# Value products of a pair in one group at beat 4, and another order of the side work, in a fused FFN, attention, FFN block

## The chip, the cores and the metric

One core of a Trainium2 chip. The metric is the device time of one launch in microseconds; smaller is better. The compute engines are TensorE (PE, and PEld for its weight loads), VectorE (DVE), ScalarE (ACT) and GpSimd (POOL); SyncE (SP) issues the DMAs.

## What is computed

Sixteen batches of 512 tokens with 128 channels go through a block of three stages, all in float32:

```python
x = x + 0.5 * ffn(layernorm(x), W_fc, W_proj)
x = x + attention(layernorm(x), w_qkv, w_out, b_out)
x = x + 0.5 * ffn(layernorm(x), W_fc, W_proj)
# attention: 16 heads of 64, q scaled by 1/8, a causal mask, sim - slope[head] * (i - j), softmax
# ffn: y = square(relu(x @ W_fc.T)) @ W_proj.T, then a spiking recurrence on y:
for step in range(5):
    mem = 0.9 * mem + y - (mem > 1)     # mem starts as y
    count += (mem > 1)
return count / 5
```

Layer norm has no weights (eps 1e-5); the output is 16 x 512 x 128 float32.

## The kernel before, in words

Heads are handled in pairs, eight pairs to a batch. The program of every engine is a sequence of *slots*, one for each pair (s = 0 to 7), and a slot has six *beats* (k = 0 to 5). "(s,k)" below means beat k of slot s. Batch 0 and batch 15 are written out; batches 1 to 14 are a hardware loop over two batches, whose body starts with the odd one (`run`, L252).

**In slot s TensorE does three pairs at once.** For pair s it makes the masked score tiles, one beat each (`scores`, L347; TILES, L26: beats 0 and 2 are 512 keys wide, 1 and 3 are 384, beats 4 and 5 hold two tiles of both heads). For pair s-1 it transposes the normalised probabilities in five runs of four 128x128 blocks (`turn`, L363; TBEAT: beats 1, 2, 3, 5, 5). For pair s-2 it makes the value products (`pv`, L378): for each block j of 128 keys, head 0 in array columns 0 to 63 and head 1 in columns 64 to 127, each of (4 - j) * 128 moving columns, all of a pair summed in one PSUM bank. PV (L40) says at which beats. A float32 product is two matmul instructions here, so one j is four of them.

**Side work** is everything else for TensorE: q and k of the next pair, v, the transposes after a layer norm (t1, t2, t3), the two FFN products of the next batch's first FFN (fc1, y1) and of the last batch's second FFN (fc3, y3), and the output projection of the last batch (out). SIDE (L65) lists it as (slot, beat, kind, tile, batch offset). Entry n of the list goes to side bank n % 2. `last_user` (L237) finds for entry n the entry before it with the same parity, and `freed` (L222) names the semaphore that says that the bank has been emptied; `side` (L451) waits for it before the first matmul. 

**Order within a beat k of slot s**, on each engine in program order:

- TensorE (`slot`, L475): the scores of tile k (they wait until VectorE has biased tile k-3, three score banks), the value products of this beat, the transposes of this beat (they wait for POOL's normalisation of the tiles concerned), then the side work of (s,k).
- VectorE (`slot`, L719): waits for the scores of tile k, then the reciprocal of the sums of tile k-2, `bias_max` of tile k (L553), then `low_half` (L666) for the side work of the beat *before*: for q, k, t it subtracts the rounded high half from the bank and stores the low half, for out it adds the residual. Then `steps` (L688): layer norm statistics and normalisation (LN1, LN2, LN3), and the steps of the spike recurrence (SPIKE1, SPIKE3).
- ScalarE (`slot`, L863): `high_half` (L819) for the side work of the beat before (q, k, t: the rounded high half; v, fc, y: the copy out of the bank), the copies of this beat's transposes (`turned_out`, L805), the copy of the finished value products at ATTBEAT (`att_out`, L812), then the exponentials of tile k (`exps`, L789).
- POOL (`slot`, L926): the multiplication of tile k-2 with the reciprocals (`norm`), and the squares of fc tiles.

So the bank of a v, fc or y is free after ScalarE's copy at the next beat; the bank of a q, k, t or out after VectorE's `low_half` at the next beat, which stands behind the wait for that beat's scores:

```python
if exists(b, s):
    bias_wait(b, s, k)          # dve.wait_ge(s_scores, tile_no(b, s, k))
last = (b, s, k - 2) if k >= 2 else (*before(b, s, 1), BEATS + k - 2)
if exists(*last[:2]):
    recip(*last)
if exists(b, s):
    bias_max(b, s, k)
...
for n, kind, i, off, ss in side_at(s, k - 1, offsets):
    low_half(n, kind, i, b + off, ss, (par + off) % 2)
steps(b, s, k, par, offsets)
```

SyncE copies the halves of q and k between partitions as soon as they are there (`place`, L289), for the pair of the next slot.

Of the kernel before, what the change touches and what calls it, by code (L numbers as in the profile page):

```python
# [35 lines left out]
TNEEDS = [max(SEG_TILE[h, i] for h, j in runs for i in range(j, NT)) for runs in TRUNS]  # L36
TRING = 8
TBEAT = [1, 2, 3, 5, 5]
ATTBEAT = 4
PV = [[2], [], [1, 3], [], [0], []]  # L40
PVORDER = [j for js in PV for j in js]

PVLAST = [max(PVORDER.index(j) for _, j in runs) for runs in TRUNS]
# [12 lines left out]
def beats_from(slot, beat, counts):  # L56

    at = [divmod(slot * BEATS + beat + n, BEATS) for n in range(len(counts))]
    return [x for x, c in zip(at, counts) for _ in range(c)]
# [3 lines left out]

SIDE = [  # L65
# [11 lines left out]
]  # L77

SPIKE1 = beats_from(3, 0, [2, 3, 1, 1, 0, 0, 1, 1, 1, 1, 2, 1])
SPIKE3 = beats_from(6, 3, [1, 2, 2, 1, 2, 1, 2, 1, 2])  # L80
LN1 = dict(stats=(0, 0), aggregate=(0, 1), rstd=(0, 1), normalise=(0, 3))
LN2 = dict(stats=(5, 2), aggregate=(5, 3), rstd=(5, 3), normalise=(6, 1))
LN3 = dict(stats=(3, 4), aggregate=(3, 5), rstd=(3, 5), normalise=(4, 0))

def macaron_kernel(nc: bass.Bass, x, w_qkv, w_out, b_out, w_fc, w_proj, out):
    ctx = ExitStack()
    with ctx:
# [251 lines left out]
        def _(pe):  # L340
# [134 lines left out]
            def slot(b, s, par, offsets, between=None):  # L475
                t_of, pv_of = before(b, s, 1), before(b, s, 2)
                for k in range(BEATS):
                    if exists(b, s):
                        scores(b, s, k, par)
                    for j in PV[k]:  # L480
                        if exists(*pv_of):
# [65 lines left out]
        def _(dve):  # L547
# [140 lines left out]
            def steps(b, s, k, par, offsets):  # L688

                if 1 in offsets:  # L690
                    nb, npar = b + 1, 1 - par
                    if (s, k) == LN1["stats"]:
                        dve.wait_ge(s_xin[npar], (nb - npar) * 8 + 16)
                        stats_of(1, x_in[:, npar, :, :], nb)
                    if (s, k) == LN1["normalise"]:
                        normalise(1, x_in[:, npar, :, :], nb)
                    for n in range(spike_ops):
                        if (s, k) == SPIKE1[n]:
                            spike_step(1, nb, n)
                    if (s, k) == SPIKE1[spike_ops]:  # L700
                        finish1(nb, npar)
# [4 lines left out]
                if -1 in offsets:  # L706
# [4 lines left out]
                    for n in range(spike_ops):  # L711
                        if (s, k) == SPIKE3[n]:
                            spike_step(3, b - 1, n)
                    if (s, k) == SPIKE3[spike_ops]:
                        finish3(b - 1)

            AGGREGATE = [(LN1["aggregate"], 1, 1), (LN3["aggregate"], 3, -1), (LN2["aggregate"], 2, 1)]

# [69 lines left out]
        def _(act):  # L788
# [74 lines left out]
            def slot(b, s, par, offsets):  # L863
                for k in range(BEATS):
                    for n, kind, i, off, ss in side_at(s, k - 1, offsets):
                        high_half(n, kind, i, b + off, ss, (par + off) % 2)
                    for t in range(len(TRUNS)):
                        if TBEAT[t] == k and exists(*before(b, s, 1)):
                            turned_out(*before(b, s, 1), t)
                    if k == ATTBEAT and exists(*before(b, s, 2)):  # L870
                        att_out(*before(b, s, 2), par if s >= 2 else 1 - par)
# [119 lines left out]
```

## Time and profile before

| | us |
|---|---|
| median of 3 runs | 1767.83 (1766.23 to 1768.95) |
| span of the profiled execution | 1764.1 |
| TensorE busy | 1676.8 (95%) |
| ScalarE busy | 1289.0 (73%) |
| VectorE busy | 1206.1 (68%) |
| POOL busy | 920.2 (52%) |
| TensorE on the chain that ended last | 69% |
| VectorE on it | 19% |

Matmuls overlap in the trace: one with 512 moving columns is shown 0.40 us long and adds 0.23 to a stream. How long a piece of work really takes on TensorE is therefore read from where one piece ends and the next ends, as in the chain of waits, and not from the length of an instruction.

### The profile page before, as it was taken

How to read it: one execution, taken by the hardware profiler on the slowest of the kernel's cores; microseconds unless marked ns; L12 is line 12 of the kernel's file. 1: busy time of each engine (PE TensorE's matmuls, PEld its weight loads, DVE VectorE, ACT ScalarE, POOL GpSimd, SP SyncE).
4: the chain of work that ended last, by engine and by line, in shares of the span. 5: the costliest groups of instructions: out<-in, count | busy, mean ns of one | idle time of the engine just before them, and what ended most of it. 6: DMA issues, size and time to landing. Idle time of an engine off the chain costs nothing.

```text
span 1764.1 us, 39796 instructions
## 1 busy us (share of the span) xinstructions
PE 1676.8 (95%) x10902; PEld 1259.1 (71%) x10902; DVE 1206.1 (68%) x4272; ACT 1289.0 (73%) x3446; POOL 920.2 (52%) x1258
## 2 busy tenths in 40 slices
PE   4899999999999999999999999999999999999996
PEld 3767777677776777767777676776777677677775
DVE  6575776748777585775858768586785848767563
ACT  2687876777877787876877768687777868868781
POOL 2455554555545455545555545465454545546451
PEclk8999999999999999999999999999999999999998
DMA  2555453435434435443545434444443544434430
GB/s 73 114 109 111 85 119 75 102 82 109 101 81 107 89 84 108 92 104 76 105 93 107 96 82 107 90 87 107 90 103 78 109 95 94 102 82 101 94 82 13
DMA packets 80562, 164.80 MB, mean 93 GB/s; under 512 B 12880, under 2 KB 30928, under 8 KB 80208
## 3 DMA queue, kind: packets, MB, share of 16 engines
q1 hardware_dynamic: 80336, 162.12, 42.9%
q8 instruction: 101, 1.65, 0.4%
q14 instruction: 125, 1.02, 0.2%
HBM read 6.88 MB, written 4.19 MB: 6 GB/s over the span
## 4 chain that ended last, share of the span: by engine, by line
PE 69%; DVE 19%; issue 8%; POOL 2%; ACT 1%; DVEq 1%; DMA 1%; SPq 0%; POOLq 0%; ACTq 0%
PE bank L388 12%; PE bank L373 12%; PE bank L343 7%; PE bank L359 7%; PE bank L431 7%; PE bank L360 6%; PE bank L439 6%; PE bank L345 5%; PE bank L344 5%; DVE spikes L615 3%; DVE negsc L558 3%; DVE negmem L621 2%; DVE drive L618 2%; DVE xn L591 1%; DVE rsum L567 1%
## 5 line engine op out<-in xcount | busy, mean ns | idle before, releaser
L911 POOL TENSOR_TENSOR prob<-prob,rsum 128x512 f32<-128x512 f32 (+3 forms) x1024 | 731.7, 730 | 699.9 <-DVE rsum L567 699.6
L799 ACT ACTIVATE prob<-negsc,negmax 128x512 f32<-128x512 f32 (+3 forms) x1024 | 574.4, 565 | 124.2 <-DVE negmax L558 117.7
L810 ACT COPY probT<-bank 128x512 f32<-128x512 f32 x640 | 362.0, 587 | 194.5 <-PE bank L373 191.9
L558 DVE CUSTOM_DVE_ANT_0 negsc<-bank,alibi 128x512 f32<-128x512 f32 (+3 forms) x1024 | 466.2, 473 | 5.3 <-PE bank L360 5.3
L567 DVE RECIPROCAL rsum<-sums 128x1 f32<-128x1 f32 (+1 forms) x768 | 121.4, 158 | 483.3 <-PE bank L360 466.3
L373 PE MATMUL bank<-ident,prob 128*128 128x128 f32 x2560 | 373.6, 277 | 1.9 <-ACT probT L810 0.2
L359 PE MATMUL bank<-keys,queries 128*128 128x256 f32 (+2 forms) x1024 | 352.1, 355 | 23.1 <-DVE negmax L558 14.4
L388 PE MATMUL bank<-probT,vals 128*64 128x256 f32 (+3 forms) x2048 | 361.0, 453 | 0.3 <-ACT attT L817 0.3
L373 PEld LDWEIGHTS bank<-ident,prob 128*128 128x128 f32 x2560 | 296.2, 141 | 39.4 <-issue 28.6
L360 PE MATMUL bank<-keys,queries 128*128 128x256 f32 (+2 forms) x1024 | 321.2, 325 | 0.0
L359 PEld LDWEIGHTS bank<-keys,queries 128*128 128x128 f32 x1024 | 194.8, 190 | 74.6 <-DVE negmax L558 30.5
L388 PEld LDWEIGHTS bank<-probT,vals 128*64 128x64 f32 x2048 | 113.0, 135 | 155.9 <-issue 106.0
L360 PEld LDWEIGHTS bank<-keys,queries 128*128 128x128 f32 x1024 | 195.4, 191 | 13.9
L799 ACT ACTIVATION_READ_ACCUMULATOR prob<-negsc,negmax 128x1 f32 x1024 | 199.3, 195 | 0.0
L917 POOL TENSOR_TENSOR hid<-hid 128x512 f32<-128x512 f32 x128 | 136.4, 1077 | 13.8 <-ACT hid L852 13.8
L431 PEld LDWEIGHTS bank<-wproj,hid 128*128 128x128 f32 x1024 | 120.7, 195 | 17.4 <-issue 12.9
L431 PE MATMUL bank<-wproj,hid 128*128 128x128 f32 x1024 | 127.4, 280 | 3.5 <-POOL hid L917 3.5
L615 DVE SCALAR_TENSOR_TENSOR spikes<-negmem,spikes 128x512 f32<-128x512 f32 (+1 forms) x136 | 117.4, 868 | 1.0
L439 PE MATMUL bank<-wo,attT 128*128 128x128 f32 x960 | 114.5, 275 | 0.0
L439 PEld LDWEIGHTS bank<-wo,attT 128*128 128x128 f32 x960 | 110.7, 192 | 0.0
L817 ACT COPY attT<-bank 128x512 f32<-128x512 f32 x128 | 74.9, 585 | 46.0 <-PE bank L388 43.5
L672 DVE TENSOR_TENSOR queries<-bank,queries 128x512 fp32r<-128x512 f32 x128 | 87.4, 683 | 15.6 <-ACT queries L827 14.9
(82 smaller groups left out, 2246.3 us busy)
## 6 DMA issues: line engine op xcount, KB each, us to landing
queries<-queries SPq DMA_DIRECT2D x384, 256.0 KB, 3.0
keys<-k_lo SPq DMA_DIRECT2D x256, 128.0 KB, 2.4
keys<-keys SPq DMA_DIRECT2D x128, 128.0 KB, 3.7
x_in<-in_L_attn_x_dram SPq DMA_DIRECT2D x16, 256.0 KB, 2.9
out_dram<-x SPq DMA_DIRECT2D x16, 256.0 KB, 2.4
prob<-in_L_attn_w_qkv_dram SPq DMA_DIRECT2D x1, 1536.0 KB, 9.1
wo<-in_L_attn_w_out_dram SPq DMA_DIRECT2D x1, 512.0 KB, 10.7
probT<-in_L_ffn_W_fc_dram SPq DMA_DIRECT2D x1, 256.0 KB, 3.2
```

The source lines that it names most:

```text
L359: pe.matmul(dst, q_hi[:, p % 2, h, rows], keys[:, p % 2, h, 0:width], start=True, stop=False)
L360: mm = pe.matmul(dst, q_lo[:, p % 2, h, rows], keys[:, p % 2, h, 0:width], start=False, stop=True)
L373: mm = pe.transpose(turn_bank[n % 2][:, col:col + P], prob[:, p % 2, h, PCOL[i] + j * P:PCOL[i] + (j + 1) * P], ident[:, :])
L388: mm = pe.matmul(pv_bank[h * DH:(h + 1) * DH, j * P:N], vals[:, (p // 2) % 2, j, (p % 2) * P + h * DH:(p % 2) * P + (h + 1) * DH], probT[: ...
L431: mm = pe.matmul(dst[:, t * C:(t + 1) * C], hid[:, i, rows], wproj[:, i, :], start=(i == 0 and t == 0), stop=(i == FC - 1), skip_group_che ...
L439: mm = pe.matmul(dst[:, 0:C], attT[:, att_at(m, par), t * P:(t + 1) * P], wo[:, m, :], start=(m == 0), stop=(m == PAIRS - 1))
L558: ins = dve.tensor_tensor_reduce(negsc[:, k % 3, col:col + WIDTH[i]], src, alibi[:, 2 * p + h, N - WIDTH[i]:N], 1.0, MASKED, ALU.add, ALU.min,
L567: dve.reciprocal(rsum[:, p % 2, cols], sums[:, p % 2, cols]).then_inc(s_rsum, 1)
L615: ins = dve.scalar_tensor_tensor(out=spikes[:, cols], in0=mem[:, cols], scalar=sign * THRESHOLD, in1=spikes[:, cols], op0=fires, op1=ALU.add)
L799: ins = act.activation(prob[:, p % 2, h, PCOL[i]:PCOL[i] + WIDTH[i]], negsc[:, k % 3, col:col + WIDTH[i]], ACT.Exp, bias=negmax[:, p % 2, ...
L810: act.copy(probT[:, turn_slot(p, t), :], turn_bank[(len(TRUNS) * p + t) % 2][:, :]).then_inc(s_turned_out, 1)
L911: ins = pool.tensor_tensor(pr, pr, rsum[:, p % 2, seg:seg + 1].to_broadcast([P, WIDTH[i]]), ALU.mult)
```

## The change

All value products of a pair move to beat 4, in the order of j, and the copy of their sum moves to beat 5. SIDE is written anew: the same kinds and numbers of side products (43 entries before and after), at other beats and in another order; with it move the beats of the layer norms' and the spikes' steps on VectorE and POOL. Sizes, banks, semaphores and arithmetic stay.

```diff
-ATTBEAT = 4
-PV = [[2], [], [1, 3], [], [0], []]
+ATTBEAT = 5
+PV = [[], [], [], [], [0, 1, 2, 3], []]
 SIDE = [
-    (0, 0, "q", 0, 0), (0, 1, "k", 0, 0), (0, 3, "v", 0, 0), (0, 4, "t1", 0, 1), (0, 4, "v", 1, 0),
-    (1, 0, "q", 0, 0), (1, 1, "k", 0, 0), (1, 2, "fc1", 0, 1), (1, 4, "fc1", 1, 1), (1, 4, "fc1", 2, 1),
-    (2, 0, "fc1", 3, 1), (2, 0, "q", 0, 0), (2, 1, "out", 0, -1), (2, 1, "out", 1, -1), (2, 2, "y1", 0, 1),
-    (2, 2, "k", 0, 0), (2, 3, "out", 2, -1), (2, 4, "y1", 1, 1), (2, 5, "v", 0, 0),
-    (3, 0, "v", 1, 0), (3, 0, "q", 0, 0), (3, 1, "k", 0, 0), (3, 2, "out", 3, -1),
-    (4, 0, "k", 0, 0), (4, 0, "q", 0, 0), (4, 2, "t3", 0, -1), (4, 3, "v", 0, 0), (4, 4, "v", 1, 0),
-    (5, 0, "q", 0, 0), (5, 1, "fc3", 0, -1), (5, 2, "k", 0, 0), (5, 4, "fc3", 1, -1), (5, 4, "fc3", 2, -1),
-    (5, 5, "fc3", 3, -1),
-    (6, 0, "q", 0, 0), (6, 1, "k", 0, 0), (6, 2, "y3", 0, -1), (6, 2, "y3", 1, -1), (6, 3, "t2", 0, 1),
-    (6, 4, "v", 0, 0), (6, 5, "v", 1, 0),
-    (7, 0, "q", 0, 1), (7, 1, "k", 0, 1),
+    (0, 0, "q", 0, 0), (0, 1, "k", 0, 0), (0, 2, "v", 0, 0), (0, 5, "v", 1, 0), (0, 5, "t1", 0, 1),
+    (1, 0, "q", 0, 0), (1, 0, "fc1", 0, 1), (1, 1, "k", 0, 0), (1, 1, "fc1", 1, 1), (1, 2, "fc1", 2, 1),
+    (1, 3, "fc1", 3, 1), (1, 5, "y1", 0, 1),
+    (2, 0, "q", 0, 0), (2, 1, "y1", 1, 1), (2, 1, "k", 0, 0), (2, 2, "out", 0, -1), (2, 3, "out", 1, -1),
+    (2, 5, "out", 2, -1),
+    (3, 0, "q", 0, 0), (3, 0, "out", 3, -1), (3, 1, "k", 0, 0), (3, 2, "v", 0, 0), (3, 3, "v", 1, 0),
+    (4, 0, "q", 0, 0), (4, 1, "k", 0, 0), (4, 2, "v", 0, 0), (4, 2, "t3", 0, -1), (4, 3, "v", 1, 0),
+    (4, 5, "fc3", 0, -1),
+    (5, 0, "q", 0, 0), (5, 0, "fc3", 1, -1), (5, 1, "k", 0, 0), (5, 2, "fc3", 2, -1), (5, 3, "fc3", 3, -1),
+    (5, 4, "t2", 0, 1), (5, 5, "y3", 0, -1),
+    (6, 0, "q", 0, 0), (6, 0, "y3", 1, -1), (6, 1, "k", 0, 0), (6, 2, "v", 0, 0),
+    (7, 0, "v", 1, 0), (7, 0, "q", 0, 1), (7, 1, "k", 0, 1),
 ]
-SPIKE1 = beats_from(3, 0, [2, 3, 1, 1, 0, 0, 1, 1, 1, 1, 2, 1])
-SPIKE3 = beats_from(6, 3, [1, 2, 2, 1, 2, 1, 2, 1, 2])
-LN1 = dict(stats=(0, 0), aggregate=(0, 1), rstd=(0, 1), normalise=(0, 3))
-LN2 = dict(stats=(5, 2), aggregate=(5, 3), rstd=(5, 3), normalise=(6, 1))
-LN3 = dict(stats=(3, 4), aggregate=(3, 5), rstd=(3, 5), normalise=(4, 0))
+SPIKE1 = beats_from(2, 3, [1, 1, 2, 1, 1, 0, 1, 1, 1, 0, 1, 1, 2, 1])
+SPIKE3 = beats_from(6, 2, [1, 1, 2, 1, 2, 1, 2, 1, 2, 1])
+LN1 = dict(stats=(0, 0), aggregate=(0, 1), rstd=(0, 1), normalise=(0, 2))
+LN2 = dict(stats=(4, 5), aggregate=(5, 0), rstd=(5, 0), normalise=(5, 2))
+LN3 = dict(stats=(3, 2), aggregate=(3, 3), rstd=(3, 3), normalise=(4, 0))
```

## Rows read from the trace of the kernel before

**Rows 1.** The page: busy time of each engine, and the chain by engine.
```profile
PE 1676.8 (95%) x10902; PEld 1259.1 (71%) x10902; DVE 1206.1 (68%) x4272; ACT 1289.0 (73%) x3446; POOL 920.2 (52%) x1258
PE 69%; DVE 19%; issue 8%; POOL 2%; ACT 1%; DVEq 1%; DMA 1%; SPq 0%; POOLq 0%; ACTq 0%
```

**Rows 2.** Windows, batches 5, 6: length; busy PE, PEld, DVE, ACT, POOL; PEclk, DMA.
```profile
558.33:665.70 107.37, 102.78 (x676) 76.84 (x676) 74.97 (x265) 80.11 (x215) 57.05 (x79) 1.00 0.44 95
665.70:770.96 105.26, 103.17 (x677) 76.78 (x676) 74.85 (x265) 80.09 (x215) 57.04 (x79) 1.00 0.45 96
```

**Rows 3.** The same for slots 0, 4 and 7 of batch 6.
```profile
665.70:679.15 13.45, 11.90 (x76) 8.19 (x75) 11.96 (x47) 10.91 (x32) 8.12 (x12) 1.00 0.63 141
...
722.01:734.05 12.04, 11.50 (x76) 8.19 (x75) 11.70 (x39) 9.70 (x27) 6.81 (x10) 1.00 0.35 75
...
761.25:770.96 9.71, 9.71 (x62) 6.53 (x60) 9.63 (x26) 7.54 (x20) 4.71 (x8) 1.00 0.43 89
```

**Rows 4.** The chain in slot 1 of batch 6: start, length, engine, line, count.
```profile
683.46 1.01 PE bank L388 x8
684.47 0.59 PE bank L373 x4
...
686.10 0.44 PE bank L373 x4
...
687.01 1.01 PE bank L388 x4
688.02 0.43 PE bank L343
688.45 0.23 PE bank L344
```

**Rows 5.** Timeline, slot 1 beat 1: start, length, engine, line, operation, shapes, count.
```profile
681.34 0.34 PE L360 MATMUL bank<-keys,queries 128*128 128x384 f32 x1
...
681.88 0.48 PE L343 MATMUL bank<-xa_hi,wk_hi 128*128 128x512 f32 x1
...
682.26 0.69 DVE L672 TENSOR_TENSOR queries<-bank,queries 128x512 fp32r<-128x512 f32 x1
```

**Rows 6.** Timeline, slot 1 beat 2: last scores matmul, low half of k.
```profile
683.06 0.40 PE L360 MATMUL bank<-keys,queries 128*128 128x512 f32 x1
...
684.17 0.69 DVE L679 TENSOR_TENSOR k_lo<-bank,keys 128x512 fp32r<-128x512 f32 x1
```

**Rows 7.** Timeline, slot 4: a side product (v 1) and what released it.
```profile
731.38 0.68 DVE L684 TENSOR_TENSOR xf_lo<-bank,xf_hi 128x512 fp32r<-128x512 f32 x1
...
732.11 0.39 PE L343 MATMUL bank<-wv_hi,xa_hi 128*128 128x256 f32 x1 [0.43 <-DVE xf_lo L684]
```

**Rows 8.** The chain in batch 8: a tile of y1.
```profile
912.48 1.79 PE bank L431 x16
```

**Rows 9.** Timeline, end of slot 1: last transposes, ScalarE's last read of beat 5.
```profile
689.92 1.03 PE L373 MATMUL bank<-ident,prob 128*128 128x128 f32 x8
...
692.28 0.20 ACT L799 ACTIVATION_READ_ACCUMULATOR prob<-negsc,negmax 128x1 f32 x1
```

**Rows 10.** Timeline of VectorE, slot 4: the normalisation before the second FFN.
```profile
724.61 2.24 DVE L591 TENSOR_SCALAR xn<-x,meanvar,rstd 128x128 f32<-128x128 f32 x4 [0.15 <-POOL rstd L924]
```

**Rows 11.** Lines by form, VectorE: busy us, mean ns of one, idle before.
```profile
L615 DVE SCALAR_TENSOR_TENSOR spikes<-negmem,spikes 128x512 f32<-128x512 f32 x120 | 111.4, 929 | 1.0
...
L649 DVE TENSOR_TENSOR x1b<-x,bias 128x512 f32<-128x512 f32 x16 | 20.5, 1280 | 0.0
```

**Rows 12.** Lines by form, POOL: normalisation of a tile 384 wide.
```profile
L911 POOL TENSOR_TENSOR prob<-prob,rsum 128x384 f32<-128x384 f32 x256 | 211.6, 827 | 305.6 <-DVE rsum L567 305.5
```

**Rows 13.** Timelines of TensorE and of VectorE at the loop's branch (batch 7).
```profile
773.07 0.49 PE L359 MATMUL bank<-keys,queries 128*128 128x512 f32 x1 [2.11 <-DVE negmax L558]
...
777.22 0.17 DVE L567 RECIPROCAL rsum<-sums 128x2 f32<-128x2 f32 x1 [2.63 <-PE bank L360]
```

**Rows 14.** Window just behind that wait: granted clock in the PEclk column.
```profile
774.20:777.60 3.40, 3.40 (x12) 2.83 (x11) 0.77 (x3) 0.00 (x0) 0.13 (x1) 0.50 0.45 123
```

## The prediction

> **What bounds the kernel now.** I read the page first: TensorE is busy for 95% of the span, and its matmuls are 69% of the chain that ended last, VectorE 19% [rows 1]. Next the windows by batch [rows 2]: an even batch takes 105.26 us, an odd one 107.37 (the loop body holds one of each; its branch lies ahead of the odd one). In either, VectorE works 75 us, ScalarE 80. Then the windows by slot of batch 6 [rows 3]: TensorE is idle in slot 0 (11.90 busy of 13.45) and slot 4 (11.50 of 12.04), in slot 7 (9.71 of 9.71) and the other five not. Last, the chain inside a slot [rows 4], where each piece ends where the next begins, so its length is what a matmul really adds. So TensorE's order of work is the bound almost everywhere, and a saving there counts in full, unless the new order makes it wait.
>
> **What the value products save.** A 128-column weight tile is followed by 64-column ones at each group. The group at beat 4 (four matmuls, two heads side by side, four passes of 512 columns at 2.4 GHz, 0.85 us) takes 1.01; the group at beat 2 (384 and 128 columns, the same 0.85) takes 1.01 too [rows 4]. So going in costs 0.15, and the change of width between products of one group costs nothing. Coming out, the next product takes 0.43 where its follower takes 0.23 (0.20 lost), and four transposes take 0.59 where four without a group ahead take 0.44 (0.15 lost) [rows 4]. The change removes the group at beat 0 (0.15 + 0.20, before a side product) and that at beat 2 (0.15 + 0.15, before transposes): 0.65 us a slot. It does so in 128 slots: 83 us, 5.2 a batch. No other TensorE work is added or dropped; the matmuls of a batch then sum to 96.0 us against 101.2 now.
>
> The Trainium skill (TensorEngine Tiling (Array Packing), Key Properties) says that a change of tiling mode drains the array, and its page TensorE: Matmul & The Clock Gate (Part 2, the drain step) puts a drain at some 128 cycles, an estimated 0.05 us at 2.4 GHz. By that, four crossings a slot would give 27 us, not 83. The trace has three to four times that at each crossing, and I go by it.
>
> **What the side work costs.** Side products use two banks in turn: each waits until the side product two places back in SIDE has been emptied (last_user, freed). For q, k, t and out it is VectorE that frees the bank, in low_half, one beat later and behind bias_max, which needs the scores of that later beat. So a side product at beat k+1 whose bank was used by a q at beat k can't start until VectorE has seen scores k+1. Length of that way: the scores of beat 1 end at 681.68 (the last starts 681.34, 0.34 long), VectorE's low half ends at 682.95 [rows 5]: 1.27 us. At beat 2: from 683.46 to 684.86, 1.40 [rows 6]. TensorE meanwhile has only four transposes (0.44) ahead of k. A released product begins 0.06 after the release and its first matmul is seen whole, 0.39 for 256 columns [rows 7] and 0.48 to 0.50 for 512 [rows 5], not the 0.12 (0.23) that it adds in a stream. So k after q: 1.27 + 0.06 + 0.50 + 0.46 = 2.29 after the scores, against 0.44 + 0.70 = 1.14 now: **1.15 us lost**. In the kernel before, k never shares q's bank at one beat's distance: in slot 1 it starts at 681.88, 0.20 after the scores end [rows 5], where the release would let it start at 683.01. In the new SIDE one entry stands between q and k, so they share. Going through the new list:
> - k at (1,1), (3,1), (5,1), (6,1), each behind q at beat 0: 4 x 1.15 = 4.6. At (2,1) k has y1 (1.79, [rows 8]) ahead and loses nothing; in slots 0, 4 and 7 its bank is another's.
> - fc1 tile 2 at (1,2) behind k at (1,1): 1.40 + 0.06 + 0.96 against 1.14 = 1.3.
> - out 3 at (3,0) behind out 2 at (2,5): its residual comes behind the bias of beat 0 (about 1.0 after the scores); q covers 0.7; with the restart 0.55.
> - Beat 5 to beat 0: here ScalarE frees the bank. After the last transpose (689.92 + 1.03) it ends beat 5 at 692.48 [rows 9], 1.5 later; the move of ATTBEAT to 5 puts another copy of 0.5 in front, and then comes the side copy, 0.5: 2.5. q at (1,0) uses the bank of v 1 at (0,5), which TensorE wants 1.6 after that transpose: with the restart 1.2 lost; fc1 tile 0 behind t1 another 0.4. fc3 tile 1 at (5,0) behind tile 0 at (4,5): 0.9. Together 2.5. y1 and y3 are longer than this and hide it.
> - Slot 4. VectorE's work of a slot is 3.7 for the tiles and 1.2 for q and k; here come the normalisation 2.24 [rows 10], t3 0.6, six spike steps at what one adds, 0.71 (a long one lasts 0.93, [rows 11]), and the last one 1.05: 13.1. Two steps leave, and stats2 with its bias addition (0.77 + 1.28, [rows 11]) comes to beat 5: 13.7, for 11.2 of TensorE. In a walk from beat to beat the low half of q ends some 4.2 after the scores of beat 0, and v 0, now at beat 2, wants its bank 1.0 earlier: 1.5 with the restart. t3 waits likewise for k: 1.3. Together 2.8; today 0.3 and 0.7 are lost there and 0.2 at slot 5.
> - Slots 6 to 0. VectorE has 4.9 + 8 x 0.75 + 0.69 = 11.6 in slot 7 for TensorE's 9.4. Slot 6 shrinks from 14.7 to 11.2 (a y3, t2 and a v leave), so the lag is carried further: when TensorE wants transpose run 0 of slot 0, its reciprocal is just starting and POOL needs 0.83 more [rows 12]: 1.8. v 0, now at beat 2, then waits for the low half of q: 0.9. Together 2.7. Today some 2.3 are lost in slot 0 of even batches, 1.5 of it at t1 behind normalise; that wait goes, since t1 moves to (0,5).
>
> Sum: 4.6 + 1.3 + 0.55 + 2.5 + 2.8 + 2.7 = 14.4 us of waits a batch, where an even batch loses 105.26 - 101.2 = some 4 now (3.65 counted wait by wait). New batch 96.0 + 14.4 = 110.4, against some 104.85 from scores to scores now (96 for 101.2, 14.4 for 3.65): +5.6.
>
> **Odd batches.** At the branch VectorE stands still for 2.63 us, and TensorE waited 2.11 on it [rows 13]. I let this surcharge stand as it is; bounds: nothing (hidden by the waits) to 1.5 us more for each of 7 branches. DMAs of q and k go out from SP as before, up to a slot ahead of their use; k of slots 2, 4 and 5 goes out one beat earlier or later with a slot to spare: nothing. The later PV copy (beat 5) frees the one PV bank a slot ahead of its next use: nothing. The new wait of ScalarE's turn copies on the value products of beat 4 is met before it comes: nothing.
>
> **Sum.** 14 inner batches x 5.6 = 78. Batch 0: six groups' saving -3.9, waits in slots 1, 3, 5, 6 7.5, t1's wait gone -1.0: +2.6. Batch 15 has no fc1: +2.4. Tail, two value products: -1.3. Together +82 on the profiled 1764.1: 1846; the median lies 3.7 above that execution: **1850**.
>
> **Rivals.**
> - *Faster: the product saving shows and the bank waits don't*, because VectorE's low halves at (1,1), (3,1), (5,1) and (6,1) are there before TensorE is through the transposes; it decides as soon as all waits together grow by less than 5.2 a batch: 1768 - 83 = 1685. For: VectorE has 30% idle. Against: its low half can't be sooner than the scores in front of it, and rows 5 and 6 show it already waiting for them. 0.10.
> - *The direct waits come, the late stretches of VectorE don't grow* (slots 4 and 0 lose what they lose today): 15 x 1.85 less, 1822. For: each new wait gives VectorE time to catch up. 0.25.
> - *Half of the direct waits are covered*: some 1775 with both signs near. 0.08.
> - *The clock falls more often.* After TensorE's 2.1 us wait at the branch the granted clock stood at 0.50 (1.2 GHz) for 3.4 us [rows 14], 1.7 us of work lost. Were that so once in each batch and not in half of them, +14; twice, +40: 1864 to 1890. For: waits of 1 to 2 us are now spread over six slots. Against: the 0.4 to 0.9 us waits of slots 0 and 4 leave it at 1.00 [rows 2]. 0.10.
> - *Merging saves nothing* (the crossing is paid within the group): 1933. The group of 384 and 128 speaks against it. 0.02.
> Four k products behind q and the one fc1 behind k cost 5.9 a batch; they alone eat the 5.2.
>
> **How the numbers follow.** Forecast 0.45 at 1850 (own range 1830 to 1868). With the second and fourth rival 0.80, which needs 1795 to 1885. Faster by over 0.2% (what a measurement of this kernel tells from no change): 0.10 and a third of the 0.08: 0.13; within 0.2%: 0.02; slower 0.85.
>
> **What would show it.** In the profile after: the sixteen value products of a slot in one stretch of 2.3 us at beat 4; TensorE's idle ahead of the side products of line 343 released by VectorE's lines 672 and 679, some 5 times a batch, 0.9 to 1.3 each; the same by ScalarE's vals and hid copies at the start of slots 1 and 5; the wait of xn at t1 gone. Batches of 110 and 113 us. I am wrong if TensorE's busy time falls by 83 and no wait of lines 672 and 679 appears, or if VectorE is found far ahead at (s,1).

## The result and the profile after

The changed kernel takes 1869.99 us (1868.32 to 1876.38), the kernel before 1767.03 (1765.58 to 1768.95): 1.059 times, 95% interval 1.0572 to 1.0609, so 103 us slower. The profiled execution of after has a span of 1867.5 us against 1764.1. Lines of the kernel after stand one further than those of before: the value products are L389, the transposes L374, the side product's first matmul L344, the low halves L673 (q) and L680 (k).

The page of the kernel after, busy time and chain by engine:

```profile
PE 1632.5 (87%) x10902; PEld 1295.6 (69%) x10902; DVE 1196.8 (64%) x4272; ACT 1305.8 (70%) x3446; POOL 929.8 (50%) x1258
PE 69%; DVE 13%; issue 9%; ACT 7%; DMA 1%; DVEq 1%; ACTq 0%; SPq 0%; POOL 0%
```

Against [rows 1] TensorE is 44 us less busy in a span 103 longer (less than the 83 saved, since the first matmul after a wait is shown whole: some 160 waits ahead of line 344, listed below, at 0.50 - 0.23 each come to an estimated 43); 7% of the chain is now ScalarE's, which had 1%. The windows of batches 5 and 6, then slots 0, 1, 4 and 7 of batch 6 (length; busy PE, PEld, DVE, ACT, POOL; PEclk, DMA share, GB/s):

```profile
586.94:700.47 113.53, 99.91 (x676) 79.38 (x676) 74.23 (x265) 81.24 (x216) 57.89 (x79) 1.00 0.42 89
700.47:811.50 111.03, 100.12 (x677) 79.31 (x676) 74.14 (x265) 81.25 (x216) 57.85 (x79) 1.00 0.43 91
700.47:713.89 13.42, 11.44 (x76) 8.72 (x76) 10.88 (x44) 11.36 (x33) 7.79 (x12) 1.00 0.70 156
713.89:731.29 17.40, 14.24 (x88) 10.63 (x87) 6.08 (x25) 12.71 (x34) 9.62 (x12) 1.00 0.33 70
760.74:773.89 13.15, 11.70 (x79) 9.13 (x78) 12.28 (x40) 10.89 (x29) 6.87 (x9) 1.00 0.43 91
801.30:811.50 10.20, 9.62 (x65) 7.20 (x63) 10.13 (x27) 8.00 (x22) 5.56 (x8) 1.00 0.38 80
```

VectorE and ScalarE have the work they had in [rows 2], and both batches are 6 us longer. Slot 1 idles for 3.2 of 17.4 us while VectorE is busy for 6.08: VectorE isn't short of time there, TensorE waits on a chain. Here is that chain around beats 1 and 4 of slot 1 (start, length, engine, what, line), to be set beside [rows 4]:

```profile
718.00 0.09 DVE negsc L559
...
718.15 0.30 issue
718.46 0.08 DVE negmax L559
718.54 0.61 DVE queries L673
719.15 0.04 issue
719.20 0.50 PE bank L344
719.70 0.23 PE bank L345
...
725.72 2.31 PE bank L389 x16
728.02 0.32 PE bank L360
728.34 0.12 PE bank L361
```

The sixteen value products take 2.31 us, for 1280 columns in four passes. A group of 512 columns took 1.01 [rows 4]; so 768 columns more took 1.30, 512 columns are worth 0.87, and 0.14 is left for the entry, which is paid once for all four blocks. The next product pays 0.20 (0.32 against 0.12) once. Above it stands the price: the bank of q is freed at 719.15, behind the bias of tile 1. TensorE's own timeline shows the idle time in brackets, with its releaser:

```profile
715.29 0.50 PE L344 MATMUL bank<-xa_hi,wq_hi 128*128 128x512 f32 x1 [0.91 <-ACT vals L834]
...
716.60 0.47 PE L344 MATMUL bank<-xf_hi,wfc_hi 128*128 128x512 f32 x1 [0.34 <-DVE xf_lo L685]
...
719.20 0.50 PE L344 MATMUL bank<-xa_hi,wk_hi 128*128 128x512 f32 x1 [0.89 <-DVE queries L673]
...
722.77 0.50 PE L344 MATMUL bank<-xf_hi,wfc_hi 128*128 128x512 f32 x1 [1.02 <-DVE k_lo L680]
```

And the view of waits of TensorE over the whole kernel (us in total, times, longest):

```profile
PE bank L344 <- DVE queries L673: 85.7, 96, 2.3
PE bank L344 <- ACT vals L834: 23.9, 32, 1.3
PE bank L344 <- DVE k_lo L680: 15.3, 15, 1.0
...
PE bank L416 <- DVE k_lo L680: 13.1, 15, 0.9
PE bank L344 <- ACT hid L853: 12.6, 18, 0.7
```

These five are 150.6 us; the view of before has no group of them above 1 us. They are idle time only: with the restart of the first matmul (0.50 where a stream adds 0.23) each wait costs some 0.3 more. That is 96 waits on the low half of q, six a batch.

### The profile page after: what moved, and what is told of

Read it like the earlier page. It is cut to its first block, busy times and chain, and to the rows that moved or that the text cites. A ratio compares the mean times of both kernels' runs of the same rounds, so it can differ in the third digit from the quotient of the medians.

```text
span 1867.5 us, 39684 instructions
## 1 busy us (share of the span) xinstructions
PE 1632.5 (87%) x10902; PEld 1295.6 (69%) x10902; DVE 1196.8 (64%) x4272; ACT 1305.8 (70%) x3446; POOL 929.8 (50%) x1258
## 4 chain that ended last, share of the span: by engine, by line
PE 69%; DVE 13%; issue 9%; ACT 7%; DMA 1%; DVEq 1%; ACTq 0%; SPq 0%; POOL 0%
PE bank L389 15%; PE bank L374 11%; PE bank L360 8%; PE bank L361 7%; PE bank L344 6%; PE bank L432 6%; PE bank L440 6%; PE bank L346 4%; PE bank L345 4%; ACT prob L800 3%; DVE queries L673 3%; DVE negsc L559 2%; DVE xn L592 1%; PE bank L416 1%; DVE k_lo L680 1%
## 5 line engine op out<-in xcount | busy, mean ns | idle before, releaser
L374 PE MATMUL bank<-ident,prob 128*128 128x128 f32 x2560 | 366.9, 274 | 12.3 <-POOL prob L912 11.5
L360 PE MATMUL bank<-keys,queries 128*128 128x256 f32 (+2 forms) x1024 | 356.6, 359 | 21.0 <-DVE negmax L559 13.4
L374 PEld LDWEIGHTS bank<-ident,prob 128*128 128x128 f32 x2560 | 305.4, 141 | 46.8 <-issue 14.1
L389 PE MATMUL bank<-probT,vals 128*64 128x512 f32 (+3 forms) x2048 | 303.9, 439 | 1.3 <-ACT attT L818 1.3
L389 PEld LDWEIGHTS bank<-probT,vals 128*64 128x64 f32 x2048 | 135.9, 136 | 155.7 <-issue 112.9
L918 POOL TENSOR_TENSOR hid<-hid 128x512 f32<-128x512 f32 x128 | 135.7, 1062 | 12.9 <-ACT hid L853 12.9
L344 PE MATMUL bank<-xa_hi,wk_hi 128*128 128x512 f32 x128 | 62.8, 490 | 70.5 <-DVE queries L673 61.8
L440 PE MATMUL bank<-wo,attT 128*128 128x128 f32 x960 | 119.1, 277 | 5.5 <-DVE x L657 5.5
L828 ACT CAST keys<-bank 128x512 fp32r<-128x512 f32 x128 | 75.5, 590 | 47.9 <-PE bank L346 47.8
L344 PE MATMUL bank<-wv_hi,xa_hi 128*128 128x256 f32 x256 | 83.0, 324 | 24.7 <-DVE queries L673 23.9
```

The source lines that it names most:

```text
L344: pe.matmul(dst, w_hi, m_hi, start=True, stop=False)
L360: pe.matmul(dst, q_hi[:, p % 2, h, rows], keys[:, p % 2, h, 0:width], start=True, stop=False)
L374: mm = pe.transpose(turn_bank[n % 2][:, col:col + P], prob[:, p % 2, h, PCOL[i] + j * P:PCOL[i] + (j + 1) * P], ident[:, :])
L389: mm = pe.matmul(pv_bank[h * DH:(h + 1) * DH, j * P:N], vals[:, (p // 2) % 2, j, (p % 2) * P + h * DH:(p % 2) * P + (h + 1) * DH], probT[: ...
L440: mm = pe.matmul(dst[:, 0:C], attT[:, att_at(m, par), t * P:(t + 1) * P], wo[:, m, :], start=(m == 0), stop=(m == PAIRS - 1))
L918: pool.tensor_tensor(hid[:, i, :], hid[:, i, :], hid[:, i, :], ALU.mult).then_inc(s_hid[w], 1)
```

## How the waits are counted below

"Wait" is what one piece of TensorE's work (a score tile, a run of transposes, a side product) takes from the end of the piece ahead to its own end, less what the same piece adds in a stream. "Work" is the rest of the batch, the crossings into and out of value products included. Work that a low clock makes longer is counted as wait too: in before and after no even inner batch has more than 0.3 us of it, in e3 each has 3 to 10 us at a granted clock of 0.50, in e6 3 to 7. An even inner batch is then, in us:

| | before | after |
|---|---|---|
| work | 101.3 | 96.1 |
| waits | 3.6 | 14.9 |
| sum, length from scores to scores | 104.9 | 111.0 |

Odd batches behind the loop's branch (3 to 13) carry what it costs besides: 2.9 before, 3.5 after.

## The experiments

All twelve kernels do the whole computation. Ratios, and differences to before in the text, are to the kernel before as run beside each (1764.8 to 1767.0 us). "Inner batch" is the mean of batches 1 to 14 between their first score matmuls, from the trace.

| kernel | median us | ratio (95%) | inner batch | waits, even batch |
|---|---|---|---|---|
| before | 1767.0 | 1 | 106.0 | 3.6 |
| after | 1870.0 | 1.059 (1.057 to 1.061) | 112.3 | 14.9 |
| e1 grouping alone | 1803.2 | 1.022 (1.021 to 1.024) | 108.3 | 11.3 |
| e2 order alone | 1865.4 | 1.056 (1.054 to 1.058) | 111.9 | 9.6 |
| e3 low halves first | 1894.3 | 1.072 (1.070 to 1.074) | 113.5 | 16.6 |
| e4 one k behind q | 1780.5 | 1.009 (1.008 to 1.011) | 107.1 | 4.8 |
| e6 all at beat 2 | 1819.2 | 1.029 (1.027 to 1.031) | 109.7 | 13.4 |
| e7 two groups | 1776.0 | 1.005 (1.004 to 1.007) | 106.6 | 7.1 |
| e8 two k later | 1836.7 | 1.039 (1.037 to 1.041) | 110.0 | 12.9 |
| e9 own order | 1767.7 | 1.000 (1.000 to 1.001) | 105.7 | 9.0 |
| e10 value copy early | 1853.1 | 1.050 (1.048 to 1.051) | 111.3 | 14.0 |
| e11 own order 2 | 1753.0 | 0.992 (0.990 to 0.994) | 105.0 | 8.0 |
| e12 own order 3 | 1744.9 | 0.989 (0.986 to 0.991) | 104.4 | 7.3 |
| e13 as e12, split | 1805.4 | 1.025 (1.021 to 1.029) | 108.0 | 5.2 |

### The two halves of the change

e1 is the kernel before with the grouping alone; e2 is the kernel after without it.

```diff
 e1, on before:
-ATTBEAT = 4
-PV = [[2], [], [1, 3], [], [0], []]
+ATTBEAT = 5
+PV = [[], [], [], [], [0, 1, 2, 3], []]
 e2, on after:
-ATTBEAT = 5
-PV = [[], [], [], [], [0, 1, 2, 3], []]
+ATTBEAT = 4
+PV = [[2], [], [1, 3], [], [0], []]
```

> The kernel before with the value products of a pair in one group at beat 4 and ATTBEAT 5, its own SIDE and steps kept. Theory (the saving of the group is real, and the new side order gives it back through the bank waits): the crossings fall by 5.2 us a batch as in the changed kernel; under the old SIDE the rule of the two banks gives new waits only where a value group had stood between (out 0 at (2,1) 0.8, y1 0 at (2,2) 0.85, q at (3,0) 0.85, slot 4 behind VectorE 2.8 in place of 0.8, slot 0 about as now): +4.2. Together -1.0 a batch: 1752, between 1735 and 1765. Rival (the long stretch of value products itself starves VectorE and ScalarE, so the group is what costs): slower than before, 1800 or more. Rival (the saving is not real): 1767 plus the 4.2 a batch, 1830.

> The changed kernel with the value products back at beats 0, 2 and 4 and ATTBEAT 4: the new SIDE and steps alone. Theory (bank waits): the four k products behind q still wait, 1.15 us each a batch; the waits at beats 0 and 2 (fc1 tile 2, out 3, fc3 tile 1, v and t3 of slot 4) find the value groups of those beats as cover and all but go. Waits of some 6.5 a batch for 3.65 before: +2.9 a batch, 1810, between 1790 and 1830. Rival (the group is what costs, the side order is harmless): 1767 within 5.

Both theories were wrong. Grouping alone costs 38 us instead of gaining 15; the new order alone costs 100, nearly all of the loss, and the grouping on top of it 3 (by the differences to before) to 5 (between the medians): an even batch saves 5.2 us of crossings and has 5.3 more of waits (9.6 to 14.9). Both steps move ScalarE's copy of the products to beat 5 as well; e10 below separates that for the new order. Two timeline lines of TensorE in e1 show the new waits, at beat 2 of slot 1 and beat 1 of slot 2, and a line of its waits the second of them over the kernel:

```profile
694.93 0.50 PE L343 MATMUL bank<-xf_hi,wfc_hi 128*128 128x512 f32 x1 [0.49 <-DVE queries L672]
...
705.63 3.84 PE L439 MATMUL bank<-wo,attT 128*128 128x128 f32 x32 [0.62 <-ACT hid L852]
```

```profile
PE bank L439 <- ACT hid L852: 8.7, 14, 0.6
```

The two value groups stood ahead of side products, at beat 0 (0.43 us of products and 0.35 of crossings) and beat 2 (0.86 and 0.30), and while they ran VectorE and ScalarE emptied the bank that comes next. In e1 eight pieces at or just behind those beats wait 0.7 to 1.0 each (fc1 0, out 0, y1 0, q of slot 3, the first transposes and t3 of slot 4, k of slot 5, y3 1). The same holds inside the new order: fc1 tile 2 waits 0.12 in e2 and 1.29 in after, out 3 nothing and 0.63, slot 4 0.65 and 1.94, fc3 tile 1 0.20 and 0.98, slot 0 about 1.4 and 2.9. All but a part of slot 0's stand behind a place where value products were. The four k at beat 1, where none ever stood, wait 1.16 in either. Products ahead are not always cover enough, and this is where e2's expectation (6.5 us of waits, 9.6 measured) failed: q and fc1 tile 0 of slot 1 wait 1.08 and 0.58 in even batches of e2 though a value product stands ahead of them, and k of slot 7 waits 1.07.

### The wait of k on the bank of q

e4 is the kernel before with one entry moved, so that one stands between q and k of slot 1 and they share a bank. e8 is the kernel after with the k of slots 3 and 6 a beat later, and v 1 of slot 3 two beats later.

```diff
 e4, on before:
-    (1, 0, "q", 0, 0), (1, 1, "k", 0, 0), (1, 2, "fc1", 0, 1), ...
+    (1, 0, "q", 0, 0), (1, 0, "fc1", 0, 1), (1, 1, "k", 0, 0), ...
 e8, on after:
-    (3, 0, "out", 3, -1), (3, 1, "k", 0, 0), (3, 2, "v", 0, 0), (3, 3, "v", 1, 0),
+    (3, 0, "out", 3, -1), (3, 2, "k", 0, 0), (3, 2, "v", 0, 0), (3, 5, "v", 1, 0),
-    (6, 0, "y3", 1, -1), (6, 1, "k", 0, 0),
+    (6, 0, "y3", 1, -1), (6, 2, "k", 0, 0),
```

> The kernel before with one entry of SIDE moved: fc1 tile 0 from (1,2) to (1,0) behind q, so that k at (1,1) shares its bank with q at (1,0) as in the changed kernel. Value products, steps and everything else as before. Theory: one wait of 1.15 us ahead of k in each of 15 batches and nothing else, 17 us: 1784, between 1781 and 1787. Rival (VectorE has a third of its time free, so an earlier wait is made good later, or something hides it): 1767 within 3.

> The changed kernel with k of slots 3 and 6 moved from beat 1 to beat 2 (and v 1 of slot 3 from beat 3 to beat 5, so that it doesn't wait in turn). Theory: two waits of 1.16 us a batch go and nothing comes; where TensorE then reaches slot 7 earlier, VectorE's lag there gives up to 1.16 of it back: 1870 less 20 to 39, 1840, between 1828 and 1852. Rival (VectorE's and ScalarE's load is what bounds the changed kernel): 1865 to 1872.

Both came out as expected: +15.3 us (0.5 under the stated range) and -33.3. TensorE in e4 at k of slot 1, and the line of waits of e4 and of e8:

```profile
687.98 0.50 PE L343 MATMUL bank<-xa_hi,wk_hi 128*128 128x512 f32 x1 [0.89 <-DVE queries L672]
```

```profile
PE bank L343 <- DVE queries L672: 14.2, 16, 0.9
```

```profile
PE bank L344 <- DVE queries L673: 48.1, 52, 1.9
```

One shared bank is sixteen waits of 0.89, with the restart 1.16 each in the count of waits, and an inner batch of e4 is 1.1 longer; the two k of e8 fell from 1.16 to 0.26, and v 0 of slot 4 behind the first of them from 0.82 to 0.37. The wait comes from the list's parity alone and costs the same with a value group ahead of q (e4) or without (after).

### Can the release come earlier?

e3 puts VectorE's low halves of a beat ahead of its wait for the scores, in the kernel after. e10 puts ScalarE's copy of the value products at beat 4, behind the exponentials.

```diff
 e3: VectorE's slot, low halves first
+                    for n, kind, i, off, ss in side_at(s, k - 1, offsets):
+                        low_half(n, kind, i, b + off, ss, (par + off) % 2)
                     (the wait for the scores, recip, bias_max)
-                    for n, kind, i, off, ss in side_at(s, k - 1, offsets):
-                        low_half(n, kind, i, b + off, ss, (par + off) % 2)
 e10: ScalarE's slot, att_out from ahead of exps to behind it, with
-ATTBEAT = 5
+ATTBEAT = 4
```

> The changed kernel with VectorE's low halves of the beat before put ahead of its wait for this beat's scores and ahead of the bias; all work is the same. Theory (what k waits for is VectorE's wait for the scores and its bias, not its work as such): the waits of k behind q (4.6 us a batch), of fc1 tile 2 (1.3) and of out 3 (0.6) go, those on ScalarE's copies stay: 1870 less 98, 1772, between 1760 and 1800. Rival (VectorE is late through its load or through ScalarE's copy of the high half, its order does not matter): above 1850. Rival (the burst of value products): no change, 1865 to 1875.

> The changed kernel with one part of the change undone: ScalarE's copy of the value products stands at beat 4 again, but behind the exponentials of that beat (so it waits for the products while TensorE hasn't reached beat 5), not at beat 5 between the turn copies and the exponentials. Theory: ScalarE then ends a slot 0.5 us earlier after the last transpose (1.5 and not 2.0), and the waits that hang on its first copies of the next slot shorten by that: q of slot 1 1.18 to 0.7, fc3 tile 1 0.98 to 0.5, k of slot 7 by some 0.2; 1.1 to 1.5 a batch, 1850, between 1842 and 1858. Rival (the place of the copy is free, ScalarE has 30% idle): 1867 to 1873.

e3 was slower by 24 us, where 98 were expected to go. Its waits of VectorE, and two lines of VectorE's timeline in slot 1:

```profile
DVE k_lo L680 <- ACT keys L828: 153.7, 127, 1.8
DVE queries L673 <- ACT queries L828: 121.9, 114, 3.1
```

```profile
721.52 0.69 DVE L673 TENSOR_TENSOR queries<-bank,queries 128x512 fp32r<-128x512 f32 x1 [0.57 <-ACT queries L828]
...
724.20 0.69 DVE L680 TENSOR_TENSOR k_lo<-bank,keys 128x512 fp32r<-128x512 f32 x1 [1.16 <-ACT keys L828]
```

The low half needs ScalarE's high half, which stands behind the exponentials of the beat before, and those need VectorE's bias. Put first, the low half blocks VectorE for 276 us in all, and the bias behind it comes late. TensorE's waits of e3 show that the wait that was aimed at went, and another grew (in after they are 23.9 and 85.7). The page's line of busy times stands below them:

```profile
PE bank L344 <- ACT vals L834: 64.4, 46, 2.7
...
PE bank L344 <- DVE queries L673: 18.9, 31, 2.5
```

```profile
PE 1677.8 (88%) x10902; PEld 1335.6 (70%) x10902; DVE 1239.2 (65%) x4272; ACT 1301.5 (69%) x3446; POOL 957.8 (50%) x1258
```

In all TensorE stands idle for 220.7 us, 14 less than in after (235.0). What makes e3 slower lies in its busy time, 45 us more for the same matmuls, at a mean granted clock of 0.953 where after has 0.987. So e3 shows a release path over two engines, each cut making the other visible, and it doesn't show that this path costs the 24 us; what brought the clock down, and what e3 would take at the clock of after, stays open.

e10 did what was expected: -17 us, q of slot 1 from 1.18 to 0.77, fc3 tile 1 from 0.98 to 0.49, k of slot 7 from 0.85 to 0.66. It also says what grouping is worth in the change's order when the copy isn't moved: e10 and e2 differ in PV and in the copy standing behind or ahead of the exponentials of beat 4, and e10 is 12 us faster (1853.1 against 1865.4; 5.2 of crossings, 4.4 of new waits a batch). The 3 to 5 us that grouping costs between e2 and after come with the later copy. How much of e1's 38 is that copy no run shows.

### Where to put a group in the old order

```diff
 on before, e6:
+ATTBEAT = 3
+PV = [[], [], [0, 1, 2, 3], [], [], []]
 on before, e7:
+ATTBEAT = 5
+PV = [[], [], [1, 3], [], [0, 2], []]
```

> The kernel before with all value products at beat 2 (ATTBEAT 3) instead of beat 4; SIDE and steps as before. As many crossings as in e1_group_only, 5.2 us a batch fewer than before. Theory (the value groups of beats 0 and 2 were the cover of bank waits): the waits that e1_group_only has at beat 2 (fc1 0.7, y1 0.9, t3 1.0, k of slot 5 0.8, y3 1.1, transposes 0.8, together 5.3 a batch) are covered again, those at beats 0 and 1 (out 0.9, q of slot 3 0.9, transposes of slot 4 0.7, slot 0) stay, t1 and v of slot 4 lose the group of beat 4 (1.5 to 2): 96.1 + 8 = 104 a batch, 1755, between 1735 and 1770. Rival (what costs is the length of the group, which starves the other engines wherever it stands): 1800, as e1_group_only.

> The kernel before with the value product of beat 0 moved into the group of beat 4 (PV at 2 and 4, ATTBEAT 5), SIDE and steps as before: one crossing in and one out fewer in a slot, 2.8 us a batch. Theory of cover: beat 2 keeps its cover, beat 0 loses it (out, q of slot 3 and transposes of slot 4 wait as in e1_group_only, 2.5 together, and slot 0 some 1 us longer): 98.5 + 6.2 = 104.7 a batch, 1762, between 1750 and 1775. Rival (long group starves): between before and e1_group_only by length, 1785.

e6 took 1819.2, 64 us over the theory and 19 over the rival, e7 1776.0, 1 over its range. In e6 the waits at beat 2 went as expected, but TensorE now waits elsewhere: the first transposes of slot 4 (2.4), out 0 (1.2), the first scores and t1 of slot 0. Its waits by POOL and ScalarE:

```profile
PE bank L373 <- POOL prob L911: 34.6, 28, 2.1
...
PE bank L439 <- ACT hid L852: 13.6, 14, 1.0
```

In before the first of these is 0.2 us in all. A part of e6's time is the clock: its mean was 0.973, before's 0.984. e7 keeps the products at beat 2 and saves 2.8 us a batch; 3.5 of waits come, at beat 0 and 1 and in slot 4: 10 us slower than before. The rival of e1, e6 and e7, a long group that starves the other engines, isn't excluded by these times; the waits that come and go with the products at beat 2 (fc1 0, y1 0, t3, k of slot 5) speak for cover, and e12 below shows that the group doesn't make a kernel slow in every order.

### Orders laid out for the grouped kernel

e9, e11 and e12 keep the group at beat 4 (e11 and e12 with e10's copy, e9 with the copy at beat 5 as in after) and lay the side work out by three rules: nothing short stands between q and k in the list, so that they take different banks; what follows beat 5 has a bank that was freed early; VectorE's steps stand in beats without low halves. Below is e12's list. In e9 t1, fc3 tile 2, y3 and the steps stand otherwise (t1 at slot 0 beat 4, y3 at beats 1 and 2 of slot 6); in e11 t1, fc3 tile 2, the last v 1 (slot 7 beat 0) and the steps:

```diff
 e12, on after (slots 1 to 6 of SIDE):
+    (1, 0, "q"), (1, 1, "k"), (1, 2, "fc1", 0), (1, 3, "fc1", 1), (1, 4, "fc1", 2), (1, 4, "fc1", 3),
+    (2, 0, "q"), (2, 1, "y1", 0), (2, 1, "k"), (2, 2, "y1", 1), (2, 3, "out", 0), (2, 3, "out", 1), (2, 5, "out", 2),
+    (3, 0, "q"), (3, 1, "k"), (3, 2, "out", 3), (3, 3, "v", 0), (3, 4, "v", 1),
+    (4, 0, "q"), (4, 1, "k"), (4, 2, "v", 0), (4, 3, "v", 1), (4, 4, "t3"),
+    (5, 0, "q"), (5, 1, "k"), (5, 2, "fc3", 0), (5, 3, "fc3", 1), (5, 3, "fc3", 2), (5, 4, "fc3", 3), (5, 5, "y3", 0),
+    (6, 0, "q"), (6, 1, "y3", 1), (6, 1, "k"), (6, 3, "v", 0), (6, 4, "t2"), (6, 5, "v", 1),
+LN1: normalise (0,4); LN2: stats (5,3), sums (5,4), normalise (5,5); LN3: stats (3,4), sums (4,1), normalise (4,3)
 e13, on e12:
-PV = [[], [], [], [], [0, 1, 2, 3], []]
+PV = [[2], [], [1, 3], [], [0], []]
```

> Value products in one group at beat 4 as in the changed kernel, with a SIDE of our own: no entry stands within a beat of the one whose bank VectorE frees unless at least 1 us of products lies between, nothing stands at beat 0 behind a bank that ScalarE frees from beat 5, t3 and the normalisations stand where the group of beat 4 covers them, and the spike steps lie at the long beats. Theory: the saving of 5.2 a batch comes through; waits of some 4 to 5 a batch are left, two of them VectorE's lag at slot 0: 96.1 + 4.5 = 100.6, 1703, between 1690 and 1740. Rival (grouping itself starves the other engines): above 1767.

> e9_own_order with the waits that its trace still names taken out by order alone: the value copy at beat 4 as in e10_att_early; the statistics of LN3 and LN2 aggregated where POOL does not hold back the normalisation of tile 3 for them (4,1) and (5,1), which made transposes of slots 4 and 6 wait 1.4 and 0.5; y3 one beat-group earlier (5,5) and (6,1), so that the third FFN's spike steps start at (6,2) and VectorE's lag at slot 0 falls by about 2; a v from slot 6 to slot 7. Theory (every wait has its own cause in the order, and the grouped products are worth their 5.2 a batch once they are gone): 96.1 + 3.5 to 5 a batch, 1697, between 1680 and 1725. Rival (the other engines' load gives back whatever is removed): 1750 to 1768.

> The second order of my own with the value products grouped, once more: tile 1's transposes of the next layer at slot 0 beat 5 again, the first norm's normalise one beat earlier, the third tile of fc3 one beat later, the second norm's statistics, sums and normalise of a layer one beat later each, and the last look at the beats that hold side work laid out anew. All work is there. Theory (TensorE's work is 96.1 us a batch, as in the grouped kernels so far, and the waits named are taken away): the waits of fc3 tile 3 (1.5 us a batch), of the third norm (1.2) and of slot 0 (2.8, half of it) go, so some 5 us of wait a batch are left of 8.0, which is 1753 less 14 x 3 = 1712 us (1700 to 1735). Rival (the load on VectorE and ScalarE as a whole sets it, and a wait removed comes back at the next hand-over): 1745 to 1755 us, as the order before it.

> The same kernel as the other one of this call, with the value products of a pair in three groups again (tile 2 at beat 0, tiles 1 and 3 at beat 2, tile 0 at beat 4), everything else in its place. All work is there. Theory (the work saved by grouping is real, and in an order that doesn't lean on the cover of these products most of it stays): 5.2 us a batch of crossings come back, less about 1.5 to 2.5 us of waits that the products at beats 0 and 2 cover, so 40 to 60 us over the other kernel. Rival (as in the two kernels with the change's own order, the cover is worth as much as the crossings): within 10 us of the other kernel.

e12's expectation names some of its steps wrongly: against e11, fc3 tile 2 stands one beat earlier and not later, the first norm's normalise two beats later and not one earlier, and the second norm's statistics and sums three beats later and not one.

The order, steps included, is worth 102 us between after and e9 and 108 between e10 and e12, at the same matmuls. But each expectation was too low by 33 to 65 us: e9 missed what POOL sets (TensorE's view of waits, e9):

```profile
PE bank L374 <- POOL prob L912: 38.8, 46, 1.9
```

In e11 and e12 those went and others came. In e12, TensorE and POOL at the end of slot 5:

```profile
742.48 0.71 PE L432 MATMUL bank<-wproj,hid 128*128 128x128 f32 x4 [1.07 <-POOL hid L918]
```

```profile
738.60 2.04 POOL L918 TENSOR_TENSOR hid<-hid 128x512 f32<-128x512 f32 x2
740.60 0.83 POOL L912 TENSOR_TENSOR prob<-prob,rsum 128x384 f32<-128x384 f32 x1
741.38 1.04 POOL L918 TENSOR_TENSOR hid<-hid 128x512 f32<-128x512 f32 x1
```

The last square of fc3 stands behind two others and a normalisation, and y3 waits for it (1.8 us a batch). e12 took 1744.9, inside the rival's 1745 to 1755 by rounding and far from the 1712 of my theory; its waits fell by only 0.7 of the 3 a batch. That the load as a whole sets this floor isn't shown by that: the waits that are left have names, y3 among them. e12 is the fastest kernel here, 1.1% under before.

e13 measures what grouping is worth in e12's order: 60.5 us between the medians, 53.3 between the spans (1743.0 and 1796.3). An inner batch costs 3.6 more: 5.2 of crossings, less 2.1 (even) or 1.2 (odd) of waits. The expectation's 40 to 60 holds within the runs' scatter. Two things make this figure too large for grouping alone. A part is the clock: the four executions of e13 were at 0.982, 0.977, 0.974 and 0.970 and took 1798.4, 1801.4, 1809.5 and 1815.5, those of e12 at 0.980 to 0.987. And e12's order was laid out for the group: it leans on the long beat 4 ahead of y3. TensorE's waits for the squares, e12 and then e13:

```profile
PE bank L432 <- POOL hid L918: 21.3, 32, 1.8
```

```profile
PE bank L432 <- POOL hid L918: 38.8, 48, 1.3
```

By the count of waits y3 tile 0 waits 1.8 us a batch in e12 and 3.3 in e13; the other waits of an even batch fall by 3.6 with the split. An order without y3 at (5,5) wasn't run in both forms. Put together, grouping the value products saves the same 5.2 us a batch each time, and the waits grow by 7.7 in the old order (+38 us), 5.3 in the change's order (+3 to +5; 4.4 and -12 with the early copy), 1.2 to 2.1 net in e12's (-53 to -60).

## Why the prediction was right, and where it was off

The direction and size held: 1850 predicted, 1870 measured, in the range. Step by step, even batches:

| step | predicted | measured |
|---|---|---|
| crossings saved | 5.2 | 5.2 |
| k at (1,1), (3,1), (5,1), (6,1) | 4.6 | 1.16 + 1.16 + 1.15 + 1.15 = 4.6 |
| k in slot 7 | 0 | 0.85 |
| fc1 tile 2 at (1,2) | 1.3 | 1.29 |
| out 3 at (3,0) | 0.55 | 0.63 |
| q and fc1 at (1,0), fc3 at (5,0) | 2.5 | 1.18 + 0.58 + 0.98 = 2.7 |
| slot 4 | 2.8 | 0.82 + 1.12 = 1.9 |
| slot 0 | 2.7 | 2.9 |
| all waits | 14.4 | 14.9 |

- **The saving.** Held at 0.65 us a slot, as the group of 2.31 above shows (this excludes the fifth rival), and e12 against e13 shows that it can come through in the time. The drain that the Trainium skill gives (TensorE: Matmul & The Clock Gate, Part 2) had come to an estimated 27 us in all; the measured price of a crossing, 0.15 to 0.20, is the larger one.
- **The bank waits.** e4 and e8 show the mechanism and its price. Each direct term was within 0.2.
- **Slot 4** is where the walk was off: VectorE arrives less late than I worked out, and the term was 0.9 too large. That k of slot 7, next, was missed by 0.85 makes the sum of the waits come out closer than its terms: this part is luck. TensorE, batch 6:

```profile
764.91 0.39 PE L344 MATMUL bank<-wv_hi,xa_hi 128*128 128x256 f32 x1 [0.56 <-DVE queries L673]
...
766.78 0.66 PE L416 MATMUL bank<-ident,xn 128*128 128x128 f32 x4 [0.90 <-DVE k_lo L680]
```

- **k in slot 7** was judged free, "in slots 0, 4 and 7 its bank is another's". It is: the bank is that of v 1 at (7,0), which ScalarE frees, and that copy comes late there (e10, with ScalarE's copy of the value products out of beat 5, took 0.2 off it). "Another's" isn't "free": the prediction followed VectorE's releases at beat 1 and not this one.
- **Inner batches**: +88.5 against 78. Even ones grew by 6.0 instead of 5.6. The odd ones behind the branch grew by 6.7, as its surcharge rose from 2.9 to 3.5, inside the bound of 1.5; batch 1, with no branch ahead, by 5.9.
- **Batch 0**: 7.0 us longer from first scores to first scores, predicted 2.6. Without a last batch, out and fc3 are absent, and k of slot 3 waits twice as long. TensorE, and ScalarE ahead of it:

```profile
87.83 0.50 PE L344 MATMUL bank<-xa_hi,wk_hi 128*128 128x512 f32 x1 [2.34 <-DVE queries L673]
```

```profile
85.76 0.72 ACT L800 ACTIVATE prob<-negsc,negmax 128x512 f32<-128x512 f32 x1 [0.28 <-DVE negmax L559]
...
86.49 0.56 ACT L828 CAST queries<-bank 128x512 fp32r<-128x512 f32 x1
```

  Here the high half of q comes at 86.49, behind beat 5's copies and the exponentials, and VectorE's low half waits for it. I had measured the release by VectorE's path alone; with little TensorE work in a slot, ScalarE's is the longer one. In e3 VectorE waits on the same path in every batch. The k of slots 5 and 6 have it too.
- **Batch 15 and the end**: +11.2, predicted +1.1. Part is the same k wait; part is the value copy at beat 5, which frees the last output products later. Two waits of TensorE at the end; the first was 1.90 in the kernel before, and the last value products, which wait in the second, didn't wait there:

```profile
1820.27 2.90 PE L447 MATMUL bank<-wo,attT 128*128 128x128 f32 x12 [3.19 <-ACT attT L818]
...
1833.47 2.38 PE L389 MATMUL bank<-probT,vals 128*64 128x512 f32 x16 [1.31 <-ACT attT L818]
```

- **The head** was 3.3 us shorter in after. The thirteen other traces, whose heads are the same code, begin their first scores anywhere from 47.7 to 52.5 us, so this is scatter. The four differences, 10.5, 4.4, 10.1 and -3.3, make up the 21.5 between 1846 and the measured span of 1867.5.
- **The rivals.** The first (waits hidden) and the third are excluded by the waits above. The second (slots 4 and 0 no worse than today) gave 1822: they wait 4.8 us, 3.1 in before, so 1.7 of the 1.85 that the forecast had on top of it did come. The fourth (the clock) is excluded for this kernel: the mean granted clock is 0.987, before 0.984.
- **What the total hides.** The count gave the right total, but reading it as 83 gained by the grouping and 165 lost by the bank waits doesn't divide the change: e1 and e2 show the order alone at +100, and grouping, with its later copy, at a loss in both orders. The prediction has the vacated places only where TensorE arrives earlier ("wants its bank 1.0 earlier") and never put a price on what the products had covered; my first experiments' expectations, which took the 5.2 as a saving in any order, failed by 50 us or more each for that reason.

## What to carry to other kernels

Work that costs setup on the bound engine may still be cover: before merging pieces, list what waits behind each place that is vacated and how long its release takes, since here the same saving of 83 us was worth +38, +3 to +5 or -53 to -60 us by the order around it, and in one order +5 or -12 by the place of a copy that had moved with it. With two buffers handed out in turn, one entry put between two others decides which share, and each sharing at one beat's distance had a price (1.16 us, sixteen times 0.89 idle) that can be worked out from the release chain before anything is built. Follow a release along every engine that it needs: cutting VectorE's path (e3) only showed ScalarE's behind it. And compare the busy time and the granted clock before laying a difference to waits.

## What the hardware showed that I had not expected

In before, windows of 3 us some 2 us into batches 3, 5, ... 15 show a granted clock of 0.50 to 0.64 in five of seven, as in [rows 14]; in after all seven show 1.00, though the wait ahead of the scores is the same (2.15 and 2.28 us where I looked, in batches 7 and 3). In after it fell later, some 6 us into the batch, behind waits of slot 0: in four of the seven (batches 3, 7, 9 and 13) the clock is 0.50 for 3.4 us. Windows of 2 us in batch 3, in which TensorE is busy for 0.73, 0.89 and 2.00:

```profile
366.00:368.00 2.00, 0.73 (x5) 0.30 (x4) 1.55 (x7) 0.84 (x3) 1.18 (x2) 1.00 0.47 139
368.00:370.00 2.00, 0.89 (x6) 0.65 (x6) 1.97 (x10) 2.00 (x6) 0.89 (x2) 0.92 0.00 0
370.00:372.00 2.00, 2.00 (x10) 1.90 (x10) 1.95 (x5) 1.80 (x5) 2.00 (x4) 0.50 0.66 139
```

Waits spread over the slots did not lower the clock on the whole: with 14.9 us of them a batch its mean was 0.987, with 3.6 it was 0.984. In e3, with 16.6 by a count that has the low clock in it, it was 0.953, though TensorE's idle time is 14 us less than in after; which waits do it I didn't settle.
